# Graph attention and a mixture of experts: the router's logits out of the projections

## The chip, the cores and the metric

The kernel runs on one core of a Trainium2 chip. The metric is the device time of one execution in microseconds (us), taken as the median of several runs.

## The reference, cut to what matters

```python
edge_index = jnp.stack([src, dst])
x = x + gnn(layernorm(x), edge_index, W, att_src, att_dst, bias)
x = x + moe(layernorm(x), router_w, w1, b1, w2, b2)

def gnn(x, ...):                                   # H = 8 heads, C = 256
    h = (x @ W).reshape(N, H, C)
    a_src, a_dst = einsum('nhc,hc->nh', h, att_src), einsum('nhc,hc->nh', h, att_dst)
    e = leaky_relu(a_src[src] + a_dst[dst], 0.2)
    alpha = softmax of e over the edges of one dst
    return segment_sum(h[src] * alpha, dst).mean(axis=heads) + bias

def moe(tokens, ...):                              # 8 experts, the best 2 of each row
    logits = tokens @ router_w.T
    rw, re = top_k(softmax(logits), 2), normalised
    return sum over e of combine[:, e] * (gelu(tokens @ w1[e] + b1[e]) @ w2[e] + b2[e])
```

N = 3125 nodes of D = 256 floats, 50,000 edges sorted by dst, all in 32-bit floats. The second layernorm's mean and rstd are those of the row after the first part, x1 = x + bias + mean over heads of the projections.

## The kernel before, in words

Nodes stand in 25 tiles of 128 rows, edges in 392 blocks of 128. Blocks are sorted by dst, so the sums of a tile of nodes come from a stretch of blocks. The projection by W is put behind the sum over edges: for every node and head the kernel sums alpha times the normalised x (256 numbers), and multiplies by W once, at the end. The order of the work on each engine is written out by hand in five programs (PE, DVE, ACT, POOL, SP); semaphores tie them together. `link` chains DVE instructions that follow from one another.

**Start.** SP loads x in seven transfers (L534 to L537) and stores zeros to starts_table (L539). ACT's queue loads W and the attention vectors. DVE makes the sums of W times attention vector (sum_va, L1401), PE their mean over D (mean_va, L927), DVE subtracts it (center_va, L1411). PE turns x tile by tile (turn_x, L919), and multiplies it by va: first for src (score(0), L932), later for dst. DVE scales by the rows' rstd (scale_scores, L1416), SP stores rows and scores as node_table (L570, L573).

**Gathers and sums, 57.56 to 656.6 us.** POOL gathers the node rows of each block (L740, 392 times), and in between sends the dst scores (L793) and reads start rows (L796). DVE makes the softmax, PE adds blocks into nodes (L978), ACT takes the sums out of PSUM and stores them in agg_table. POOL's last gather ends at 608.6, the last sums at 656.6.

**Projection, 656.6 to 853.2 us.** For tile t: SP loads the raw sums (load_raw, L603, 1.6 MB into one of three buffers; it waits for over_part(t-2) and own_part(t-3), since the buffer must be free). DVE adds what neighbouring pieces share (over_part(t), L1799 and L1804), ACT copies the rest (own_part(t), L1284). PE multiplies by W: 16 products of 128x128 by 128x256 into one PSUM bank (project(t), L1103), written into a bank that add_node(t-4) has left. DVE adds the result to x (add_node, L1815) and takes statistics (L1818). After five tiles DVE normalises them (normalise, L1822 to L1836) into tn, rows that POOL later sends to the experts' lists.

PE turns the normalised rows (turn_tn, L1114), ACT copies them out of PSUM (copy_tT, L1290), and PE multiplies them by router_w (router, L1123). After five tiles DVE subtracts the row's maximum (shift_logits, L1849 and L1850), ACT takes exp (L1294), DVE picks two experts (L1857 to L1891), PE counts rows per expert (positions(q), L1131 to L1133), DVE makes places (places_in_lists, L1896 to L1907), and POOL sends the rows (L840). DVE's program in this stage, for each t, is: over_part(t+2), then picks, places, or after tile 16 the counting of the jobs, then add_node(t), then normalise if five are whole. Tiles are taken from the last to the first in x_all (rows_of(t)).

Turns and router products are spread over the projections by turned_after(t): two tiles of rows behind most projections, the rest behind the last of a five. The last five tiles' rows are turned between the first expert jobs.

**Experts, 853 to 1013 us.** 56 jobs of up to 128 rows: load rows, turn (L1150), two products (L1162, L1178), result (results(j), L2044), and POOL adds it to the output (L854). The first 11 jobs work on the rows of the first ten tiles, while the last rows are still on their way.

Of the kernel before, what the change touches and what calls it, by code (L numbers as in the profile page):

```python
# [13 lines left out]
P = 128  # L14
# [13 lines left out]
BLK = 128  # L28
# [36 lines left out]
def gat_moe_kernel(nc, x, src, dst, W, att_src, att_dst, gnn_bias, router_w, w1, b1, w2, b2, out):  # L65
# [68 lines left out]
    with ExitStack() as ctx:  # L134
# [7 lines left out]
        RING = ROOM * ROW  # L142
        ring = sb("ring", [P, RING])
        rows = ring[0:BLK, :].rearrange("p (s d) -> p s d", d=ROW)

        o = 0
        xn = ring[:, o:o + TILES * D].rearrange("p (t d) -> p t d", d=D)
        o += TILES * D
        W_in = ring[:, o:o + 2 * H * C].rearrange("p (k n) -> p k n", k=2)
        o += 2 * H * C  # L150
# [6 lines left out]
        xT = ring[:, o:o + TILES * D].rearrange("p (t d) -> p t d", d=D)  # L157
        o += TILES * D
        reach_junk, first_home_bc, last_home_bc = (ring[:, o + n * NB:o + (n + 1) * NB] for n in range(3))
        o += 3 * NB  # L160
        assert o <= RING
# [7 lines left out]
        at_raw0 = at_W + 2 * H * C  # L169
        at_x = (first_of[GROUPS - 2] + SLOT0) % ROOM * ROW  # L170
        at_agg0 = at_x + TILES * D
        assert at_w1 + 4 * D <= at_W and at_raw0 + 2 * RAW <= at_x and at_agg0 + AGG <= RING
        assert at_x <= (first_of[WHOLE - 1] + SLOT0) % ROOM * ROW + GB * ROW
        x_all = ring[:, at_x:at_x + TILES * D].rearrange("p (t d) -> p t d", d=D)
        W_sb = ring[:, at_W:at_W + 2 * H * C].rearrange("p (k n) -> p k n", k=2)
# [132 lines left out]
        va = sb("va", [P, 2, 2 * H])  # L308
# [15 lines left out]
        node_half = sb("node_half", [P, 2 * TILES])  # L324
        counted = sb("counted", [P, 2 * TILES])
        block_of = sb("block_of", [P, TILES])
        block_at = sb("block_at", [P, TILES])
# [24 lines left out]
        router_sb = sb("router_sb", [P, 2, NX])  # L352
# [48 lines left out]
        def alphas_in_bank(g):  # L401
# [19 lines left out]
        dst_ready, first_bc_done, last_row_done = sem("dst_ready"), sem("first_bc_done"), sem("last_row_done")  # L421
        xn_ready, xT_done, xT_ready, score_done, score_ready = (
# [27 lines left out]
        tr_done, tT_ready, logit_done, shift_ready, exp_ready = (  # L450
            sem("tr_done"), sem("tT_ready"), sem("logit_done"), sem("shift_ready"), sem("exp_ready"))
        in_b2, fills_ready, filled = sem("in_b2"), sem("fills_ready"), sem("filled")
        taken_ready, pos_done, slots_ready = sem("taken_ready"), sem("pos_done"), sem("slots_ready")
        logits_read = sem("logits_read")
# [19 lines left out]

        def turned_bank(t):

            return bank[4 + t % 2] if t < TILES - UNROLL else bank[(7, 5)[t % 2]]

        def turned_after(t):

            each = {t0: 2 for t0 in range(UNROLL, TILES - UNROLL)}
            done = 0
            for i in range(UNROLL, t + 1):
                whole = i // UNROLL * UNROLL
                n = min(whole - done, each.get(i, 3))
# [1655 lines left out]
```

## Time and profile before

| | |
|---|---|
| runs shown | 1019.93, 1159.93, 1015.24 us; median 1019.93 |
| span of the profiled execution | 1013.5 us |
| its mean granted TensorE clock | 0.812 |
| busy share | PE 66%, DVE 66%, POOL 65%, ACT 35% |
| first gather of node rows | 57.56 us |
| end of the gathers | 608.6 us |
| projection | 656.6 to 853.2 us |

The profiled execution is one execution of its own; its time is its span and a few microseconds around it, and the clean runs lie 1.7 and 6.4 us above that span. Times of rows are microseconds from the start of the span. PEld is the load of weights, which overlaps PE; SPq and DVEq are the sequencers of SP and DVE. A row's square bracket tells how long the engine was idle before it and what ended that.

### The profile page before, as it was taken

How to read it: one execution, taken by the hardware profiler on the slowest of the kernel's cores; microseconds unless marked ns; L12 is line 12 of the kernel's file. 1: busy time of each engine (PE TensorE's matmuls, PEld its weight loads, DVE VectorE, ACT ScalarE, POOL GpSimd, SP SyncE). 2: the span in 40 equal slices, each digit the busy share in tenths (PEclk: the TensorE clock that was granted, in tenths of full speed). 3: DMA queues.
4: the chain of work that ended last, by engine and by line, in shares of the span. 5: the costliest groups of instructions: out<-in, count | busy, mean ns of one | idle time of the engine just before them, and what ended most of it. 6: DMA issues, size and time to landing. Idle time of an engine off the chain costs nothing.

```text
span 1013.5 us, 15559 instructions
## 1 busy us (share of the span) xinstructions
PE 669.1 (66%) x3740; PEld 603.6 (60%) x3741; DVE 673.9 (66%) x1844; ACT 355.2 (35%) x831; POOL 657.5 (65%) x705
## 2 busy tenths in 40 slices
PE   3982012428546275472656678699999998678996
PEld 2981001327545275472656678688888886567995
DVE  6988318727657276573876778557768868765663
ACT  3730003347645364241332210123322232335674
POOL 5777777777777777777777770244063275557876
PEclk9555555579877797776977798799999999789998
DMA  9634153578867677565664555098985772366874
GB/s 348 212 94 95 24 119 105 165 228 266 264 201 238 214 247 225 164 194 160 186 190 136 165 174 228 29 389 311 340 334 192 289 245 71 86 130 106 133 129 58
DMA packets 96984, 189.61 MB, mean 187 GB/s; under 512 B 24743, under 2 KB 54802, under 8 KB 95804
## 3 DMA queue, kind: packets, MB, share of 16 engines
q0 software_dynamic: 31680, 70.52, 28.6%
q1 hardware_dynamic: 50256, 72.93, 21.3%
q10 hardware_dynamic: 14960, 45.16, 11.5%
q8 instruction: 34, 0.56, 0.2%
q14 instruction: 54, 0.44, 0.1%
HBM read 124.74 MB, written 64.74 MB: 187 GB/s over the span
## 4 chain that ended last, share of the span: by engine, by line
PE 29%; DVE 23%; POOL 21%; issue 12%; DMA 8%; ACT 3%; DVEq 1%; ACTq 1%; POOLq 1%; SPq 0%; PEld 0%; PEldq 0%
POOL ring L740 17%; PE banks L1103 10%; PE banks L978 8%; PE banks L1162 3%; PE banks L1178 3%; POOL starts_table L793 2%; DMA ring<-agg_table 2%; DMA ring<-node_table,idx 2%; DMA out<-ring 2%; PE banks L932 2%; DVE arena L1379 2%; DVE ring L1804 1%; DVE arena L1684 1%; ACTq L1250 1%; ACT arena L1264 1%
## 5 line engine op out<-in xcount | busy, mean ns | idle before, releaser
L740 POOL DMA_INDIRECT ring<-node_table,idx x392 | 396.6, 1012 | 121.4 <-issue 113.8
L978 PE MATMUL banks<-arena,ring 128*128 128x160 f32 x1568 | 258.2, 329 | 36.7 <-ACT banks L1270 19.1
L978 PEld LDWEIGHTS banks<-arena,ring 128*128 128x128 f32 x1568 | 246.8, 213 | 48.7 <-issue 48.5
L1264 ACT COPY arena<-banks 128x400 f32<-128x400 f32 x200 | 88.4, 493 | 312.6 <-PE banks L978 196.6
L1103 PE MATMUL banks<-ring 128*128 128x256 f32 x544 | 120.5, 381 | 0.0
L854 POOL DMA_INDIRECT out<-ring x56 | 89.8, 1603 | 33.2 <-DMA out<-ring 16.8
L1103 PEld LDWEIGHTS banks<-ring 128*128 128x128 f32 x544 | 102.5, 190 | 13.4
L1754 DVE TENSOR_TENSOR arena<-hot,banks 128x640 f32<-128x640 f32 x84 | 64.6, 814 | 37.4 <-PE banks L978 35.1
L985 PE MATMUL banks<-ident,edge_e 128*128 128x128 f32 x25 | 7.1, 415 | 111.2 <-DVEq L1655 111.2
L1162 PEld LDWEIGHTS banks<-ring 128*128 128x128 f32 x448 | 61.1, 201 | 19.0 <-DVE ring L2020 15.8
L1162 PE MATMUL banks<-ring 128*128 128x128 f32 x448 | 63.7, 288 | 12.7 <-DVE ring L2020 12.3
L985 PEld LDWEIGHTS banks<-ident,edge_e 128*128 128x128 f32 x25 | 3.9, 201 | 113.1 <-DVEq L1655 113.1
L840 POOL DMA_INDIRECT slot_table<-arena,slots x50 | 54.6, 1093 | 14.5 <-issue 13.7
L1178 PE MATMUL banks<-arena,ring 128*128 x224 | 61.7, 400 | 1.6 <-issue 1.6
L835 POOL COPY arena<-tags 128x3 f32<-128x3 f32 x25 | 3.6, 195 | 84.5 <-DVEq L1908 84.5
L1103 PE MATMUL banks<-ring,arena 128*128 128x256 f32 x256 | 57.0, 381 | 0.0
L1268 ACT COPY banks<-zeros 128x400 f32<-128x400 f32 x100 | 50.4, 504 | 11.5 <-ACT arena L1264 10.3
L1647 DVE TENSOR_TENSOR edge_z<-ring,arena 128x384 f32<-128x384 f32 (+2 forms) x9 | 4.3, 477 | 74.8 <-DMA ring<-node_table,idx 74.7
L1103 PEld LDWEIGHTS banks<-ring,arena 128*128 128x128 f32 x256 | 48.3, 190 | 6.4
L2044 DVE SCALAR_TENSOR_TENSOR ring<-banks,job_w,ring 128x256 f32<-128x256 f32 x56 | 27.1, 484 | 36.1 <-PE banks L1178 21.4
L1270 ACT COPY banks<-zeros 128x400 f32<-128x400 f32 x100 | 49.7, 497 | 0.0
L1178 PEld LDWEIGHTS banks<-arena,ring 128*128 128x128 f32 x224 | 40.2, 200 | 6.8 <-issue 2.9
(411 smaller groups left out, 1175.7 us busy)
## 6 DMA issues: line engine op xcount, KB each, us to landing
agg_table<-arena ACTq DMA_DIRECT2D x100, 400.0 KB
ring<-agg_table SPq DMA_DIRECT2D x25, 1600.0 KB, 8.5
ring<-slot_table SPq DMA_DIRECT2D x56, 130.0 KB, 2.6
ring<-node_table,idx POOLq DMA_INDIRECT x392, 3.0
ring<-in_x SPq DMA_DIRECT2D x8, 640.0 KB, 12.6
arena<-in_L_ffn_w SPq DMA_DIRECT2D x16, 256.0 KB, 8.6
node_table<-ring SPq DMA_DIRECT2D x5, 640.0 KB, 5.2
ring<-in_L_gnn_W ACTq DMA_DIRECT2D x1, 2048.0 KB, 9.1
```

Of the source, the lines that this page charges most:

```text
L740: pool.indirect_dma_start(rows[:, slot_of(b), :], None, node_table, bass.IndirectOffsetOnAxis(idx[:, b:b + 1], 0)).then_inc(got[got_of(g)] ...
L840: pool.indirect_dma_start(slot_table, bass.IndirectOffsetOnAxis(slots[:, k, t:t + 1], 0), tn[t % TN_RING], None).then_inc(sent[t % TN_RING ...
L854: pool.indirect_dma_start(out, bass.IndirectOffsetOnAxis(xs[j % XS_RING][:, D:D + 1].bitcast(I32), 0), ybuf[j % Y_RING], None, bounds_chec ...
L978: m = pe.matmul(columns[:, k, bass.ds(at * (UNIT * H), SPREAD * H)], lhs[:, k * P:(k + 1) * P], weights, start=False, stop=True, skip_grou ...
L1103: m = pe.matmul(bank[proj_bank(t)][:, 0:D], aggt[t % AGG_RING][:, k * H + h, :], W_sb[:, k, h * C:(h + 1) * C], start=(k == 0 and h == 0), ...
L1162: m = pe.matmul(h_bank[j % 2][:, f * P:(f + 1) * P], w1_now[j % 2][:, k, f * P:(f + 1) * P], xsT[j % 2][:, k, :], start=(k == 0), stop=(k ...
L1178: m = pe.matmul(y_bank[j % 2][:, 0:D], h_sb[j % 2][:, f, :], w2_sb[:, bass.ds(e, 1), f, :].rearrange("p e n -> p (e n)"), start=(f == 0), ...
L1264: act.copy(stage[j][:, k * SLOTS * H:(k + 1) * SLOTS * H], views[k]).then_inc(drained, 1)
L1268: act.copy(views[0], zeros[:, 0:1].to_broadcast([P, SLOTS * H]))
L1270: act.copy(views[1], zeros[:, 0:1].to_broadcast([P, SLOTS * H])).then_inc(acc_free, 1)
L1754: dve.tensor_tensor(spread[:, s:s + QUAD, :].rearrange("p s (d h) -> p s d h", h=H), hot[:, q * QUAD:(q + 1) * QUAD, :].unsqueeze(3).to_br ...
L2044: dve.scalar_tensor_tensor(ybuf[j % Y_RING], y_bank[j % 2][:, 0:D], job_w[j % 3][:, 1:2], b2_now[j % 3], ALU.mult, ALU.add).then_inc(y_rea ...
```

## The change

The router's logits of a normalised row are rstd * (x1 . r - mean * sum(r)), and x1 . r is x . r + bias . r + the mean over heads of (sums @ (W_h @ r)). The kernel after the change makes these three parts and no longer turns and multiplies the normalised rows:

- x . r: router_w is loaded as 8 rows (r_rows), PE turns it to rT beside va, and the score products have 16 columns in place of 8. DVE keeps the part in x_logits.
- W_h @ r: PE turns W in 32 pieces, ACT copies them, PE multiplies them by rT: 8 more columns per head, which DVE places in W_sb. Each projection then has 264 columns, and add_node adds the 8 new ones to x_logits.
- bias . r and sum(r) come from two more small products; shift_logits has three more instructions for mean and rstd.

turn_tn, router and copy_tT are gone, and with them their semaphores. router_sb is no longer loaded. W_sb is loaded in two transfers with rows of 1 KB, and load_raw(1) also waits for one more block, since its buffer lies elsewhere. Two modulo operations of PE's register work are masks now, and POOL's waits in the adding of results have one more mask. The last shift_logits stands ahead of results(0).

```diff
+            sp.dma_start(r_rows, router_w).then_inc(in_router, 16)
             sp.wait_ge(zero_ready, 1)
...
-            sp.dma_start(W_sb[:, :, :], W.rearrange("(k p) n -> p k n", p=P)).then_inc(in_proj_w, 16)
+            for k in range(2):
+                sp.dma_start(W_sb[:, k, :, 0:C], W[k * P:(k + 1) * P, :].rearrange("p (h n) -> p h n", h=H)).then_inc(in_proj_w, 16)
             load_raw(0)
+            sp.wait_ge(block_done, first_of[GROUPS - 2] + 2)
             load_raw(1)
...
+            pool.wait_ge(w_router_done, 1)
             pool.wait_ge(target_scores_stored, 16)
...
-                at_least = [pool.snap(new[j - i - 1] + (y_landed(i) - 16)) for i in ahead]
+                at_least = [pool.snap((new[j - i - 1] & 16) + (y_landed(i) - 16)) for i in ahead]
...
             def score(a, t):
+                n = (H + NX, H)[a]
                 for k in range(2):
-                    m = pe.matmul(bank[a][:, t * H:(t + 1) * H], xT[:, t, k * P:(k + 1) * P], va[:, k, a * H:(a + 1) * H],
-                                  start=(k == 0), stop=(k == 1))
+                    m = pe.matmul(bank[a][:, t * n:(t + 1) * n], xT[:, t, k * P:(k + 1) * P],
+                                  va[:, k, 0:H + NX] if a == 0 else va_of[1][:, k, :], start=(k == 0), stop=(k == 1))
...
+            pe.wait_ge(in_router, 16)
+            for k in range(2):
+                pe.transpose(bank[1][:, H + k * NX:H + (k + 1) * NX], r_rows[:, k * P:(k + 1) * P], ident[0:NX, 0:NX])
             mean_va(0)
...
+            pe.wait_ge(blocks_counted, 2 * TILES)
+            pe.wait_ge(x_logits_kept, 1)
+            W_PARTS = 2 * H * C // P
+            for i in range(W_PARTS // 4):
+                if i >= 2:
+                    pe.wait_ge(wT_ready, i - 1)
+                for n in range(4):
+                    k, c = divmod(4 * i + n, W_PARTS // 2)
+                    m = pe.transpose(bank[(0, 2)[i % 2]][:, n * P:(n + 1) * P], W_in[:, k, c * P:(c + 1) * P], ident[:, :])
+                m.then_inc(w_turned, 1)
+            for i in range(W_PARTS // 2):
+                pe.wait_ge(wT_ready, i // 2 + 1)
+                for f in range(2):
+                    pe.matmul(bank[7][:, i * NX:(i + 1) * NX], wT[:, 2 * i + f, :], rT[:, f, :], start=(f == 0), stop=(f == 1))
...
-                        mid = pe.snap((at_homes // 256) % 128 + 1)
+                        mid = pe.snap(((at_homes // 256) & 127) + 1)
...
-                        m = pe.matmul(bank[proj_bank(t)][:, 0:D], aggt[t % AGG_RING][:, k * H + h, :], W_sb[:, k, h * C:(h + 1) * C],
+                        m = pe.matmul(bank[proj_bank(t)][:, 0:CN], aggt[t % AGG_RING][:, k * H + h, :], W_sb[:, k, h, :],
...
                 project(t)
-                for i in turned_after(t):
-                    turn_and_route(i)
...
+                if a == 0:
+                    dve.tensor_copy(x_logits[:, :, :], got_scores[:, :, H:]).then_inc(x_logits_kept, 1)
...
+            dve.tensor_copy(W_sb[:, :, :, C:].rearrange("p k h e -> p (k h) e"), w_router.rearrange("p (i e) -> p i e", e=NX))\
+                .then_inc(w_router_placed, 1)
             over_part(0)
...
             results(0)
-            shift_logits(LAST_Q)
```

The order of work shows the change at three places. First PE at the end of a cycle of five, before: the last turns and router products behind one projection, then project, positions(2) and the next project (L1103 is project, L1114 the turns, L1123 the router, L1132 and L1133 positions).

```order
L1123 MATMUL banks<-router_sb,tT 128x8 [waits tT_ready]
L1123 MATMUL banks<-router_sb,tT 128x8
L1123 MATMUL banks<-router_sb,tT 128x8 [waits tT_ready]
L1123 MATMUL banks<-router_sb,tT 128x8
L1103 MATMUL banks<-ring 128x256 [waits y1_ready,agg_own,agg_over]
L1103 MATMUL banks<-ring 128x256 x15
L1103 MATMUL banks<-ring 128x256 [waits y1_ready,agg_own,agg_over]
L1103 MATMUL banks<-ring 128x256 x15
L1132 MATMUL banks<-pick_tmp,before_me 128x40 [waits taken_ready]
L1133 MATMUL banks<-taken,ones_sq 128x40
L1103 MATMUL banks<-ring,arena 128x256 [waits y1_ready,agg_own,agg_over]
```

And after the change, where L1126 is project and L1135 and L1136 are positions:

```order
L1126 MATMUL banks<-ring,arena 128x264 [waits y1_ready,agg_own,agg_over]
L1126 MATMUL banks<-ring,arena 128x264 x15
L1126 MATMUL banks<-ring 128x264 [waits y1_ready,agg_own,agg_over]
L1126 MATMUL banks<-ring 128x264 x15
L1126 MATMUL banks<-ring 128x264 [waits y1_ready,agg_own,agg_over]
L1126 MATMUL banks<-ring 128x264 x15
L1135 MATMUL banks<-pick_tmp,before_me 128x40 [waits taken_ready]
L1136 MATMUL banks<-taken,ones_sq 128x40
L1126 MATMUL banks<-ring,arena 128x264 [waits y1_ready,agg_own,agg_over]
```

Between two positions PE now has nothing but projections; its waits for tn and tT are gone, and positions still waits for taken_ready, which DVE's picks give.

Second, the start of PE's program, before: the last of the first turns of x, the mean of va, the next turns.

```order
L919 MATMUL banks<-ident,ring 128x128 [waits in_x1]
L919 MATMUL banks<-ident,ring 128x128
L927 MATMUL banks<-va,ones_sq 128x8 [waits va_summed,idx_ready,dst_ready]
L927 MATMUL banks<-va,ones_sq 128x8
L919 MATMUL banks<-ident,ring 128x128 [waits in_x1,xT_ready,va_ready]
L919 MATMUL banks<-ident,ring 128x128
```

After (L943 turns the router's rows):

```order
L917 MATMUL banks<-ident,ring 128x128 [waits in_x1]
L917 MATMUL banks<-ident,ring 128x128
L943 MATMUL banks<-ident,ring 128x8 [waits in_router,idx_ready,dst_ready]
L943 MATMUL banks<-ident,ring 128x8
L925 MATMUL banks<-va,ones_sq 128x8 [waits va_summed]
L925 MATMUL banks<-va,ones_sq 128x8
L917 MATMUL banks<-ident,ring 128x128 [waits in_x1,xT_ready,va_ready]
L917 MATMUL banks<-ident,ring 128x128
```

The two turns of router_w stand ahead of the mean, and the wait in_router with them; all that stands behind them on PE waits too.

Third, DVE in the projection stage, from an add_node (L1815, L1818) over an over_part (L1799, L1804) to the beginning of the picks (L1849), before:

```order
L1815 SCALAR_TENSOR_TENSOR ring<-banks,ring 128x256 [waits proj_done,bias_added]
L1818 BN_STATS stats<-ring 128x6 [waits y1_ready]
L1799 TENSOR_TENSOR ring<-ring 128x8x18 [waits proj_done,raw_in1,dve_chain]
L1804 TENSOR_TENSOR ring<-ring 128x8x3x18
L1799 TENSOR_TENSOR ring<-ring 128x8x18
L1804 TENSOR_TENSOR ring<-ring 128x8x3x18
L1849 TENSOR_REDUCE row<-banks 128x5 [waits logit_done]
L1850 TENSOR_TENSOR logits<-banks,row 128x40 [waits dve_chain]
```

And after, where add_node is L1812, L1814 and L1817, over_part L1796 and L1801, and shift_logits begins at L1846:

```order
L1812 SCALAR_TENSOR_TENSOR x_logits<-banks,x_logits 128x8 [waits proj_done,bias_added]
L1814 SCALAR_TENSOR_TENSOR ring<-banks,ring 128x256 [waits dve_chain]
L1817 BN_STATS stats<-ring 128x6 [waits y1_ready]
L1796 TENSOR_TENSOR ring<-ring 128x8x18 [waits proj_done,raw_in1,dve_chain]
L1801 TENSOR_TENSOR ring<-ring 128x8x3x18
L1796 TENSOR_TENSOR ring<-ring 128x8x18
L1801 TENSOR_TENSOR ring<-ring 128x8x3x18
L1846 TENSOR_TENSOR probs<-mean,rT_sum 128x40
L1847 TENSOR_TENSOR probs<-x_logits,probs 128x40 [waits dve_chain]
L1848 TENSOR_TENSOR probs<-probs,rstd 128x40 [waits dve_chain]
L1849 TENSOR_REDUCE row<-probs 128x5 [waits dve_chain]
L1850 TENSOR_TENSOR logits<-probs,row 128x40 [waits dve_chain]
```

L1812 and L1846 to L1848 are new; before, L1849 waited for logit_done of PE.

## Rows read from the trace of the kernel before

**Rows 1.** Spans and mean granted clock of the core.
```profile
core 0: 1013.5 us, clock 0.812
```

**Rows 2.** Timelines of four engines, start (start us, us, what, [idle before]).
```profile
23.02 0.58 PE L927 MATMUL banks<-va,ones_sq 128*128 128x8 f32 x4 [1.83 <-DVEq L1406]
...
18.61 0.33 SPq L539 DMA_DIRECT2D starts_table<-arena  x1
...
52.13 0.36 DVE L1416 TENSOR_TENSOR score_all<-banks,rstd 128x200 f32<-128x200 f32 x1 [2.41 <-PE banks L932]
...
57.56 1.00 POOL L740 DMA_INDIRECT ring<-node_table,idx  x1 [0.30 <-issue]
```

**Rows 3.** Windows, start (length; busy PE, PEld, DVE, ACT, POOL; clock, DMA share, GB/s).
```profile
28.00:30.00 2.00, 2.00 (x11) 2.00 (x11) 2.00 (x8) 2.00 (x8) 1.55 (x5) 0.50 0.85 277
30.00:32.00 2.00, 2.00 (x12) 2.00 (x11) 2.00 (x8) 2.00 (x9) 1.70 (x2) 0.50 0.17 55
```

**Rows 4.** Page, costliest groups, POOL's gathers.
```profile
L740 POOL DMA_INDIRECT ring<-node_table,idx x392 | 396.6, 1012 | 121.4 <-issue 113.8
```

**Rows 5.** Windows in the projection stage and behind it.
```profile
725.00:750.00 25.00, 23.90 (x121) 20.59 (x120) 19.36 (x63) 5.72 (x10) 14.63 (x23) 1.00 0.74 268
750.00:775.00 25.00, 24.89 (x124) 22.00 (x123) 18.44 (x58) 7.86 (x10) 4.32 (x11) 1.00 0.73 272
...
862.00:866.00 4.00, 3.99 (x26) 3.82 (x25) 2.61 (x13) 2.27 (x4) 3.31 (x5) 0.72 0.31 104
...
866.00:876.00 10.00, 5.32 (x24) 4.53 (x23) 7.99 (x41) 2.97 (x6) 3.04 (x8) 0.67 0.29 65
```

**Rows 6.** Timeline of PE, projection stage and its end.
```profile
722.93 7.07 PE L1103 MATMUL banks<-ring 128*128 128x256 f32 x32
...
729.84 0.31 PE L1132 MATMUL banks<-pick_tmp,before_me 128*128 128x40 f32 x2
...
738.31 0.75 PE L1114 MATMUL banks<-ident,arena 128*128 128x128 f32 x4 [0.96 <-DVE arena L1836]
...
739.68 7.15 PE L1103 MATMUL banks<-ring,arena 128*128 128x256 f32 x32
...
746.67 0.38 PE L1114 MATMUL banks<-ident,arena 128*128 128x128 f32 x2
...
747.98 7.15 PE L1103 MATMUL banks<-ring 128*128 128x256 f32 x32
...
754.97 0.38 PE L1114 MATMUL banks<-ident,arena 128*128 128x128 f32 x2
...
756.28 7.15 PE L1103 MATMUL banks<-ring 128*128 128x256 f32 x32
...
838.38 0.42 PE L1132 MATMUL banks<-pick_tmp,before_me 128*128 128x40 f32 x2 [1.39 <-DVEq L1882]
...
861.77 0.44 PE L1114 MATMUL banks<-ident,arena 128*128 128x128 f32 x2 [2.40 <-DVE arena L1836]
```

**Rows 7.** Timeline of DVE, the same stage.
```profile
746.94 0.42 DVE L1815 SCALAR_TENSOR_TENSOR ring<-banks,ring 128x256 f32<-128x256 f32 x1 [1.65 <-PE banks L1103]
...
749.61 0.74 DVE L1799 TENSOR_TENSOR arena<-ring 128x144 f32<-128x144 f32 x1 [1.78 <-DMA ring<-agg_table]
...
755.24 0.42 DVE L1815 SCALAR_TENSOR_TENSOR ring<-banks,ring 128x256 f32<-128x256 f32 x1 [1.51 <-PE banks L1103]
...
759.12 0.43 DVE L1799 TENSOR_TENSOR ring<-ring 128x144 f32<-128x144 f32 x1 [2.99 <-DMA ring<-agg_table]
...
763.19 0.20 DVE L1861 TENSOR_TENSOR pick_tmp<-probs,row 128x40 f32<-128x40 f32 x1
```

**Rows 8.** Chain of waits, end of the projection stage.
```profile
822.72 8.98 DMA ring<-agg_table
```

**Rows 9.** Timeline of PE and DVE, ahead of the reads.
```profile
109.23 0.58 PE L963 MATMUL banks<-ident,step_cols 128*1 128x128 f32 x2 [25.99 <-DVEq L1584]
...
147.32 0.17 DVE L1605 COPY arena<-start_rows 98x8 f32<-98x8 f32 x1 [34.93 <-DMA arena<-starts_table]
```

More of the change, by code:

```diff
@@ L160, in gat_moe_kernel @@
         o += 3 * NB
-        assert o <= RING
+        r_rows = ring[0:NX, o:o + D]
+        o += D
+        assert o <= RING and 2 * H * C <= SLOT0 * ROW
         AGG = 2 * H * P
@@ L473, in y_landed @@
             return 16 * (j // Y_RING + 2)
[L475 to L485, printed above, removed]
-                if i == t:
-                    return range(done, done + n)
-                done += n
-            return range(0)
         POSITIONS_AFTER = {2 * UNROLL - 1: 0, 3 * UNROLL - 1: 1, 4 * UNROLL - 1: 2, 5 * UNROLL - 3: 3}
@@ L960, in _ @@
             m.then_inc(home_bc_done, 1)
+            pe.wait_ge(blocks_counted, 2 * TILES)
[12 more added lines that the diff above has]
+                    pe.matmul(bank[7][:, i * NX:(i + 1) * NX], wT[:, 2 * i + f, :], rT[:, f, :], start=(f == 0), stop=(f == 1))
+            pe.wait_ge(bias_rows_ready, 1)
+            for k in range(2):
+                m = pe.matmul(bank[7][:, 2 * H * NX:2 * H * NX + H + NX], ones_sq[:, :], va[:, k, 0:H + NX], start=(k == 0), stop=(k == 1))
+            m.then_inc(w_router_done, 1)
             pe.wait_ge(step_cols_ready, 1)
@@ L1236, in _ @@
                 count_blocks(n)
+            for i in range(2 * H * C // (4 * P)):
+                act.wait_ge(w_turned, i + 1)
+                act.copy(wT[:, 4 * i:4 * i + 4, :].rearrange("p i n -> p (i n)"), bank[(0, 2)[i % 2]]).then_inc(wT_ready, 1)
             for h in range(H):
@@ L1514, in _ @@
             scale_scores(1)
+            dve.wait_ge(in_router, 16 * 2)
+            for k in range(2):
+                link(dve.tensor_scalar(va[:, k, 0:H], rT[:, k, :], bias_cols[:, k:k + 1], None, ALU.mult))
+            dve.sem_inc(bias_rows_ready, 1)
             link(dve.tensor_copy(extras[:, :], extra_f[:, :]))
@@ L1846, in shift_logits @@
                 tiles, r, rev = parts(q)
-                dve.wait_ge(logit_done, tiles.stop)
-                scores = bank[6][:, 0:UNROLL * NX].rearrange("p (s e) -> p s e", e=NX)
+                scores = probs[:, :, :]
+                link(dve.tensor_tensor(scores, bc(mean[:, tiles], UNROLL), rT_sum[:, :].unsqueeze(1).to_broadcast([P, UNROLL, NX]), ALU.mult))
+                link(dve.tensor_tensor(scores, x_logits[:, TILES - tiles.stop:TILES - tiles.start, :][:, ::-1, :], scores, ALU.subtract))
+                link(dve.tensor_tensor(scores, scores, bc(rstd[:, tiles], UNROLL), ALU.mult))
                 link(dve.tensor_reduce(r[0], scores, AX_X, ALU.max))
@@ L2090, in _ @@
             normalise(TILES - 2, 2)
+            shift_logits(LAST_Q)
             results(0)
-            shift_logits(LAST_Q)
             first_pick(LAST_Q)
```

122 lines of the change are left out of this document (51 added, 71 removed).

## The prediction

> **What bounds the kernel now.** I read the spans first, then the page's groups, the windows of 25 us, the timelines of PE and DVE, and last the chain of waits. The profiled execution spans 1013.5 us at a mean granted clock of 0.812 [rows 1]. There are three long stages with different limits, and the reader should see a different engine lead in each.
>
> The start, until the first gather of node rows at 57.56, is a chain: PE takes the mean of W·att at 23.02, turns x and makes the scores, which DVE scales at 52.13; they go to the node table, and POOL gathers from it [rows 2]. From there to 608.6 POOL sets the pace: 392 gathers of 1.012 us, and 113.8 of its 121.4 us of waiting are plain issue time [rows 4]. Whatever moves the start moves this whole stage.
>
> The stage from 656.6 to 853.2 projects 25 tiles (196.6 us). By busy time PE leads: 24.89 of 25 us in one window, against DVE's 18.44 [rows 5]. By waits it is less clear. In the cycle of five tiles that ends near 780 PE waits for DVE's normalised rows once, 0.96 us [rows 6]; DVE waits for PE twice (1.65 and 1.51), and right behind each it waits again, 1.78 and 2.99, for the raw sums that SP loads from agg_table [rows 7]. The chain of waits goes through such a load, 8.98 us at 822.72, then through ACT's own_part [rows 8]. SP issues raw(t) when DVE has finished over_part(t-2), and over_part(t) waits for it: a loop of DVE and DMA with no matmul in it, except through buffers that come free.
>
> **The change, part by part.**
>
> *Projection, PE.* A tile is 16 products of 256 columns: from 722.93 to 729.84, 6.91 us [rows 6]. At 264 columns it is 6.91 x 264/256 = 7.13: +0.216, over 25 tiles +5.4. What goes are turns and router products: 738.31 to 739.68, 746.67 to 747.98, 754.97 to 756.28, which is 1.37 + 1.31 + 1.31 = 4.0 per five tiles of rows, and the wait of up to 0.96 [rows 6]. Over the four cycles that is 16 of work and about 3 of waits. Were PE the bound all along, the stage would take -19 + 5.4 = -14. That is rival A.
>
> *Projection, DVE.* Each add_node gets one more instruction, 128x8 out of PSUM; each pick of five tiles gets three more of 128x40. A 128x40 takes 0.20 [rows 7]; with the gap to the next I take 0.235 for it and 0.21 for the 128x8. 5 x 0.21 + 3 x 0.235 = 1.75 per five tiles, 8.8 over the stage.
>
> *Which of them decides.* PE, lighter by 4.0 - 1.1 per cycle, runs ahead. DVE's two waits for PE shrink, but the wait for raw sums behind each grows by as much, since that load was issued behind an over_part that stands ahead of both. Once PE's lead is used up by this, DVE's work alone sets the cycle, and that grows by 1.75, of which the raw waits swallow what lies between an over_part and the next load. Walking through the cycles with these durations I get normalise(4) later by 0.8, (9) by 1.7, (14) by 3.0, (19) by 3.5; these four are estimates, and in the cycle with the job counting (after tile 16) DVE hardly waits, so nothing is swallowed. From over_part(22) on the chain is the load, own_part, exps, picks, positions(3), project(23) and (24) [rows 8]: +0.7 for the new instructions of the picks and +0.43 for two wider tiles, less some 1.1 of router work that stood between. I take +3.5; the same walk with quicker loads gives +1, with slower ones +4.5, and -14 is the lower end.
>
> *PE's new waits.* PE will stand still where it used to turn rows: some 5 us before positions(1), 3 before positions(2), 8 before positions(3), where it waited 1.39 [rows 6]. The granted clock, 1.00 in the windows of this stage, fell to 0.72 and 0.67 in 862 to 876, after PE had waited 2.40 at 861.77 [rows 5, 6]. A tile at the lower level, 1.2 GHz, takes 6.9 us longer; a stall may be followed by part of one. Behind positions(1) and (2) PE's lead hides most of it. I take +1, bounds 0 and +21.
> The Trainium skill, "TensorE: Matmul & The Clock Gate", section on HAM oscillation, says that waits between bursts of products throttle the array again, so that each next burst starts cold. The trace agrees at 862 to 876; by that rule each of the three stalls is followed by a slow stretch, which is rival C.
>
> *The start.* router_w's load goes on SP's queue where the store of starts_table stands at 18.61, ahead of that store and behind the loads of x, and PE waits for it before the mean at 23.02 [rows 2]. The DMA engines are at 0.85 at 28 to 30 and at 0.17 after it [rows 3]. The store behind it is 1.57 MB, some 5 us at 277 GB/s, so the loads of x end near 25, and these 8 KB with them: 25.5 (bounds: 21.2, which costs nothing, and 30, which costs 7). Then two turns and the copy of rT, 0.6 together: the mean's product starts near 26.1 and the scores 3.2 later. DVE copies x_logits, 128x200, 0.36 as L1416 itself takes [rows 2], ahead of the sums that POOL's gather waits for. Of the 3.5 about 1.0 may be slack between the stored scores and POOL's look-ups, and some of the turning of x can fill the wait: I take +2.2 at the first gather, and as POOL seldom waits for others until 608.6 [rows 4], +2.2 behind that stage.
>
> *Turning W.* 32 turns and 34 small products on PE, 8 copies on ACT. Two turns took 0.58 at 109.23, two small products 0.58 at 23.02: 66 x 0.29 = 19 us [rows 2, 9]. They lie in PE's idle 25.99 us before 109.23 and the stretch behind it, DVE's five small instructions in its 34.93 before 147.32 [rows 9]. POOL's new wait, ahead of the read of the start rows, comes some 30 us behind that work, with nothing on POOL delayed. Cost 0; without cover it would be 19. The copy of the router columns into W stands ahead of over_part(0), where DVE waits for PE's last blocks; W itself comes in rows of 1 KB, 50 us before its use: 0.
>
> *Register work and the end.* PE's modulo per four blocks becomes a mask, more instructions of shorter length: 0, bound 1. POOL's adding of expert outputs gets a mask per awaited job beside waits for landed data: +0.3, bounds 0 and 2. At the tail, PE's turns that waited until 861.77 are gone [rows 6], and the maximum of the logits follows the last normalise, but results(0) stands ahead of the first pick: -0.3, bounds -1.3 and 0.
>
> **Sum.** +2.2 (start) +3.5 (projection) +1 (clock) +0.3 (POOL) -0.3 (tail) = +6.7: a span of about 1020. The clean runs shown are 1015.24 and 1019.93, which is 1.7 and 6.4 above the profiled span; with 4 to 5 around it the time is 1025. Against the median shown, 1019.93, that is half a per cent more, and a measurement of this kernel tells about 2%, 20 us.
>
> **The rivals.**
> A, PE is the bound. For it: the busy shares [rows 5]. Against it: the waits for raw sums directly behind DVE's waits for PE [rows 7]. It gives -14 in the stage, +2.2 at the start and -0.3 at the tail: 1013.5 - 12 and 4.5 around it, about 1006.
> The Trainium skill, "Perfetto Trace Analysis", section Identifying the Most-Contended Engine, says to relieve first the engine of the highest occupancy, TensorE judged by its weight loads (here 22.00 of 25 us, DVE 18.44). By that page A is the likeliest case; the order of the waits makes me put it second.
> B, little moves. The router row lands early, loads are quick, the clock stays, part of PE's lead does reach DVE: 0 at the start and -4 to +1 behind it, 1014 to 1020.
> C, slower: the clock. If each of the three stalls is followed by one slow tile, +6.9 each, and PE's lead doesn't hide them, +21, with the other terms +5.7: about 1045. It decides from the point where a slow stretch outlasts the lead of 5 to 8 us. For it: the fall at 862 [rows 5]. Against it: the window of 725 to 750 kept 1.00 through the wait of 0.96 [rows 5, 6].
>
> **How the numbers follow.** Forecast (+2 to +14; 1020 to 1033) 0.56, A (1001 to 1010) 0.20, B 0.14, C 0.07, something else, such as a longer start, 0.03. The forecast stands at 1025; the range that leaves out two in ten is 1004 to 1037. Faster by over 2% (below 999.5) 0.04, slower by over 2% (above 1040.3) 0.07, within 2% 0.89.
>
> **What would show it.** Start: the first gather near 59.8. PE: a wait of several us before positions(1) and positions(3) where now there are 0 and 1.39, tiles of 7.1 us. DVE: waits for raw sums longer, waits for PE near 0. It would be wrong if the stage takes under 190 us (then A), if the first gather is at 57.6, or if the windows of the stage show a clock under 0.95 (then C).

## The result and the profile after

The kernel after takes 1022.45 us (median of 11 runs), the kernel before 1018.46 in the same series: a ratio of 1.0038, 95% interval 1.0021 to 1.0055, so some 4 us slower. One of the 11 runs of the kernel before took 1159.93 us, in a slow state; it is in the median and not in the ratio. The forecast was 1025, +6.7 over the profiled span. The profiled execution spans 1016.9 us, 3.4 more than [rows 1]. Both profiled executions are among the quickest of their kernels (by its span about 1015.2 us where the median is 1018.46, and 1018.63 where it is 1022.45), so a difference of 1 or 2 us between two profiles can be one execution's own.

The start, in the timelines of PE and POOL after the change (start us, us, what, idle before):

```profile
24.88 0.35 PE L943 MATMUL banks<-ident,ring 8*128 8x8 f32 x2 [4.23 <-DMA ring<-in_L_ffn_router_w]
25.16 1.02 PE L925 MATMUL banks<-va,ones_sq 128*128 128x8 f32 x4
...
59.75 0.94 POOL L737 DMA_INDIRECT ring<-node_table,idx  x1 [2.84 <-DVEq L1386]
```

PE waits 4.23 us for router_w, and the mean's product stands at 25.16 in place of 23.02. The first gather is at 59.75 in place of 57.56 [rows 2], +2.19. On the way there DVE scales the scores at 54.65 in place of 52.13, +2.52.

The projection stage as one window, from the first product of project to the start of the last, in the kernel before and then in the kernel after (length; busy PE, PEld, DVE, ACT, POOL; clock, DMA share, GB/s):

```profile
656.60:853.00 196.40, 191.39 (x944) 166.94 (x943) 144.74 (x442) 54.34 (x76) 82.14 (x121) 1.00 0.75 277
```

```profile
655.90:855.30 199.40, 186.92 (x824) 157.58 (x822) 153.64 (x482) 47.58 (x56) 86.25 (x123) 0.97 0.75 274
```

The reader sees three things. The stage is 3.0 us longer, though PE has 4.5 us less to do. DVE has 8.9 us more. And the stage begins at 655.9, where it began at 656.6: of the 2.2 us lost at the start nothing is left in this pair of profiles. Behind the stage 161.6 us are left, before 160.5: +1.1. So -0.7 + 3.0 + 1.1 = 3.4.

PE's waits in the stage, in its timeline after the change; they answer to the waits of 0.96 and 1.39 in [rows 6]:

```profile
766.60 0.39 PE L1134 MATMUL banks<-taken,ones_sq 128*128 128x8 f32 x2 [1.94 <-DVEq L1881]
767.29 16.17 PE L1126 MATMUL banks<-ring 128*128 128x264 f32 x64
...
807.01 0.41 PE L1135 MATMUL banks<-pick_tmp,before_me 128*128 128x40 f32 x2 [2.04 <-DVEq L1881]
807.48 9.06 PE L1126 MATMUL banks<-ring,arena 128*128 128x264 f32 x32
...
838.27 0.65 PE L1135 MATMUL banks<-pick_tmp,before_me 128*128 128x40 f32 x2 [7.43 <-DVEq L1881]
839.14 8.98 PE L1126 MATMUL banks<-ring,arena 128*128 128x264 f32 x32
```

PE stands still ahead of positions(1), (2) and (3), and the row behind each wait is 1.6 to 1.8 us longer than rows of the same length elsewhere in the stage (7.28 for one tile, 14.55 for two; 16.17 is two tiles). The granted clock behind the waits shows it, here in the 3 us behind the longest; behind the other two it is 0.56 (767 to 770) and 0.55 (808 to 811), where it was 1.00 before PE stood still:

```profile
838.00:841.00 3.00, 2.73 (x8) 2.36 (x9) 2.64 (x10) 0.00 (x0) 0.00 (x0) 0.50 0.30 80
```

At 838.27 the cause of the wait can be followed back on ACT and DVE:

```profile
831.15 1.90 ACT L1275 COPY ring<-ring 128x448 f32<-128x448 f32 x2 [10.61 <-DMA ring<-agg_table]
832.95 0.24 ACT L1281 ACTIVATE logits<-logits 128x40 f32<-128x40 f32 x1
```

```profile
828.90 0.41 DVE L1850 TENSOR_TENSOR logits<-probs,row 128x40 f32<-128x40 f32 x1
833.28 0.20 DVE L1856 TENSOR_REDUCE row<-logits 128x5 f32<-128x40 f32 x1 [3.96 <-ACT logits L1281]
```

DVE has the logits of the fourth five ready at 829.3. ACT could take their exp at once, but its program has own_part(24) first, which waits for the raw sums until 831.15. Before the change this order held DVE up almost as long:

```profile
833.83 0.20 DVE L1857 TENSOR_REDUCE row<-logits 128x5 f32<-128x40 f32 x1 [3.30 <-ACT logits L1294]
```

But PE then had turns and router products to do and waited only 1.39 us for the picks [rows 6]. positions(3) itself stands at 838.27 after the change and at 838.38 before it: PE's 7.43 us are its lead, which ends in this wait.

### The profile page after: what moved, and what is told of

Same layout as the page of the kernel before. It is cut to its first block, busy times and chain, and to the rows that moved or that the text cites. A ratio compares the mean times of both kernels' runs of the same rounds, so it can differ in the third digit from the quotient of the medians.

```text
span 1016.9 us, 16065 instructions
## 1 busy us (share of the span) xinstructions
PE 684.6 (67%) x3692; PEld 614.7 (60%) x3693; DVE 687.7 (68%) x1892; ACT 351.3 (35%) x814; POOL 654.6 (64%) x705
## 4 chain that ended last, share of the span: by engine, by line
DVE 25%; PE 24%; POOL 23%; issue 12%; DMA 9%; SPq 2%; ACT 1%; POOLq 1%; DVEq 1%; ACTq 0%; PEld 0%; PEldq 0%
POOL ring L737 20%; PE banks L1000 8%; PE banks L1126 5%; PE banks L1171 3%; PE banks L1158 3%; DMA ring<-agg_table 3%; DMA out<-ring 3%; POOL starts_table L790 2%; PE banks L931 2%; DVE ring L1801 2%; DMA ring<-node_table,idx 2%; DVE arena L1359 2%; SPq L528 1%; PE banks L1146 1%; PE banks L917 1%
## 5 line engine op out<-in xcount | busy, mean ns | idle before, releaser
L737 POOL DMA_INDIRECT ring<-node_table,idx x392 | 393.4, 1003 | 124.1 <-issue 114.5
L1000 PE MATMUL banks<-arena,ring 128*128 128x160 f32 x1568 | 261.4, 332 | 38.2 <-ACT banks L1261 18.8
L1000 PEld LDWEIGHTS banks<-arena,ring 128*128 128x128 f32 x1568 | 251.0, 216 | 49.2 <-issue 48.6
L1126 PE MATMUL banks<-ring 128*128 128x264 f32 x544 | 124.8, 390 | 1.1 <-DVE ring L1801 1.1
L1126 PEld LDWEIGHTS banks<-ring 128*128 128x128 f32 x544 | 104.0, 192 | 19.7 <-DVE ring L1801 2.0
L1158 PEld LDWEIGHTS banks<-ring 128*128 128x128 f32 x448 | 61.8, 204 | 26.2 <-DVE ring L2021 23.3
L1126 PE MATMUL banks<-ring,arena 128*128 128x264 f32 x256 | 61.7, 402 | 0.0
L1275 ACT COPY ring<-ring 128x448 f32<-128x448 f32 x30 | 28.9, 1012 | 82.8 <-DMA ring<-agg_table 82.8
L1126 PEld LDWEIGHTS banks<-ring,arena 128*128 128x128 f32 x256 | 50.8, 199 | 9.2
```

The costliest lines, as they stand in the source:

```text
L737: pool.indirect_dma_start(rows[:, slot_of(b), :], None, node_table, bass.IndirectOffsetOnAxis(idx[:, b:b + 1], 0)).then_inc(got[got_of(g)] ...
L1000: m = pe.matmul(columns[:, k, bass.ds(at * (UNIT * H), SPREAD * H)], lhs[:, k * P:(k + 1) * P], weights, start=False, stop=True, skip_grou ...
L1126: m = pe.matmul(bank[proj_bank(t)][:, 0:CN], aggt[t % AGG_RING][:, k * H + h, :], W_sb[:, k, h, :], start=(k == 0 and h == 0), stop=(k == ...
L1158: m = pe.matmul(h_bank[j % 2][:, f * P:(f + 1) * P], w1_now[j % 2][:, k, f * P:(f + 1) * P], xsT[j % 2][:, k, :], start=(k == 0), stop=(k ...
L1275: a = act.copy(to[:, k, :, :, OVER:HOME], raw[t % RAW_RING][:, :, k, OVER:HOME, :].rearrange("p v n h -> p h v n"))
```

## The experiments

They ran in four series, each on one chip with the kernel before beside it: e1, e4, e5 and e6 on one, e2, e3, e8 and e10 on another, e11 to e13 on a third, e14 on a fourth. The chips differ: beside the result and beside e11 to e13 the kernel before takes 1018 us, beside the first eight runs 1145, beside e14 1155. So I read two things of each run: the ratio to the kernel before of the same chip, and the length of the projection stage in its profile.

Each length comes from one profile. For the kernels like before it hardly depends on the chip (196.4, e5 195.3, e13 195.3). For those like after, which do the same work in this stage, it spreads more: 199.4, e1 201.5, e8 201.8, e12 202.2. Cutting the stage at the start of positions(3) shows where each run gains or loses (us):

| run | start of the stage to positions(3) | from there to the end | stage |
|---|---|---|---|
| before | 181.8 | 14.6 | 196.4 |
| e5, before with the masks | 180.7 | 14.6 | 195.3 |
| e4, e5 without the turns | 178.7 | 16.7 | 195.4 |
| e6, e5 with DVE's additions | 183.6 | 14.6 | 198.2 |
| after | 182.4 | 17.0 | 199.4 |
| e1 | 183.4 | 18.1 | 201.5 |
| e8, after again | 183.8 | 18.0 | 201.8 |
| e12 | 184.5 | 17.7 | 202.2 |
| e11, after with PE kept at work | 182.5 | 15.0 | 197.5 |

**e4 and e5: PE's relief by itself.** e5 is the kernel before with the register masks; e4 is e5 without the turns, ACT's copies and the router.

```diff
-                for i in turned_after(t):
-                    turn_and_route(i)
...
-                scores = bank[6][:, 0:UNROLL * NX].rearrange("p (s e) -> p s e", e=NX)
+                scores = tn_all[:, at:at + UNROLL, 0:NX]
```

> The kernel before with the change's register masks alone (the two modulo operations of PE per four blocks, one more mask per awaited job on POOL); nothing else differs. My theory, that the change's cost lies in the projection stage and the start: time as before, within 1.5 us, the gathers end at the same time as before (608.6 us). Rival, that the masks gave back what the start lost in the gather stage: the sums end 2 to 3 us earlier than 656.6.

> As e5, and the turns of the normalised rows, their copies on ACT and the router products are left out; DVE takes the first eight columns of the normalised rows as logits, so the routing is another one. This relieves PE exactly as the change does, without the wider products and without anything on DVE. Theory, DVE and the loads of raw sums bound the stage: 0 to -3 us, and DVE's waits for raw sums grow while its waits for PE go. Rival, PE is the bound: -14 us or more.

Measured: e5 1144.96 us, ratio 1.0014 (0.9984 to 1.0044); e4 1142.25 us, ratio 0.999 (0.9956 to 1.0024). The stage is 195.3 us in e5 and 195.4 in e4. Here are the waits of the stage (us in total, times, longest), first e5, then e4:

```profile
DVE ring L1799 <- DMA ring<-agg_table: 14.6, 6, 3.6
...
DVE ring L1815 <- PE banks L1103: 8.4, 5, 2.5
DVE arena L1799 <- DMA ring<-agg_table: 8.4, 3, 4.1
...
DVE row L1857 <- ACT logits L1294: 2.7, 4, 1.8
```

```profile
DVE ring L1784 <- DMA ring<-agg_table: 18.4, 6, 4.2
...
DVE arena L1784 <- DMA ring<-agg_table: 10.6, 3, 4.6
...
PE banks L1133 <- DVEq L1865: 8.3, 2, 8.1
...
DVE row L1840 <- ACT logits L1286: 6.3, 4, 5.2
```

DVE's wait for PE, 8.4 us, is gone. Its waits for raw sums go from 23.0 to 29.0, and that for the exp from 2.7 to 6.3: together 9.6 more. PE, with some 10 us less to do, waits for DVE instead. Rival A, -14, falls.

The unchanged length hides two things, though: e4 is 2.0 us quicker up to positions(3) and 2.1 slower behind it. There PE has waited 8.07 us, where it waited 0.26 in e5, and the next tile takes 8.89 us in place of 7.15:

```profile
963.21 0.65 PE L1133 MATMUL banks<-pick_tmp,before_me 128*128 128x40 f32 x2 [8.07 <-DVEq L1865]
963.66 0.63 PE L1134 MATMUL banks<-taken,ones_sq 128*128 128x40 f32 x2
964.09 8.89 PE L1104 MATMUL banks<-ring,arena 128*128 128x256 f32 x32
```

The granted clock of the stage is 0.96 in e4. So, by one profile against one, PE's relief is worth 2 us, and the clock takes them back. The masks by themselves cost nothing that can be measured.

**e6: DVE's additional instructions by themselves**, on e5.

```diff
                 dve.wait_ge(proj_done, t + 1)
+                link(dve.scalar_tensor_tensor(spare_logits[:, rows_of(t), :], bank[proj_bank(t)][:, 0:NX], 1.0 / H, spare_logits[:, rows_of(t), :],
+                                              ALU.mult, ALU.add))
...
+                link(dve.tensor_tensor(spares, spares, bc(mean[:, tiles], UNROLL), ALU.mult))
+                link(dve.tensor_tensor(spares, spares, bc(mean[:, tiles], UNROLL), ALU.subtract))
+                link(dve.tensor_tensor(spares, spares, bc(rstd[:, tiles], UNROLL), ALU.mult))
```

> As e5, with the change's additional DVE instructions of the projection stage alone: one 128x8 out of PSUM per add_node (25) and three of 128x40 per pick of five tiles, on a scratch of their own, results unused. Theory, DVE is in the path: +2 to +5 us. Rival, PE is the bound and DVE has room: within 1 us of e5.

Measured: ratio 1.0058 (1.0025 to 1.0092), 4.8 us above e5 by the medians; the stage 198.2, +2.9, all of it ahead of positions(3). DVE is busy 6.3 us more there (150.9 against 144.6), and the rest goes into its idle time. DVE is in the path.

**e8: the kernel after again, and e2: without the 25 additions to the logits.**

> The kernel after, unchanged, as the measure for the runs beside it, since another chip than the first one ran the last four (before: 1145.5 us). If the chip is again one on which the stage of gathers is long: theory, the projection stage is 3 to 3.5 us longer than in the kernel before (199.4 against 196.4 in the first pair), whatever the chip; what the start and the gathers do is open, and could be of either sign there.

```diff
-                link(dve.scalar_tensor_tensor(x_logits[:, rows_of(t), :], bank[proj_bank(t)][:, D:CN], 1.0 / H, x_logits[:, rows_of(t), :],
-                                              ALU.mult, ALU.add))
```

> The kernel after without the 25 additions of the projections' eight columns to x_logits (L1812): the logits lack the part of the graph attention, so the routing is another one. Theory, DVE is in the path: the stage is 1 to 3 us shorter than the kernel after's. Rival, these small instructions are hidden by the waits for raw sums: under 0.5 us.

Measured: e8 1134.87 us, and here the ratio is 0.9896 (0.987 to 0.9921): on this chip the change makes the kernel 1.0% faster. Its stage is 201.8 us, so what is gained lies ahead of it (last section). Part of what sets it apart from the first profile of the same kernel is one load of raw sums: ahead of the picks of the second five DVE waits for it 3.65 us at 874.05 in e8 and 4.13 at 762.43 in e12, where it was 2.22 at 758.14, and PE's wait for positions(1) goes from 1.94 to 3.40 and 3.88.

e2: ratio 0.9897, the stage 198.2, 3.6 shorter than e8's, where 1 to 3 were expected. With the spread between profiles of the kernel after, this supports that these additions are in the path, but does not give their price to 1 us. Its total is no lower than e8's: the last part, with another routing, takes 166.3 us against 161.6.

**e3: the exp ahead of own_part(24).**

```diff
             for t in range(TILES):
+                if t == TILES - 3:
+                    exps(TILES // UNROLL - 2)
                 if t + 2 < TILES:
                     own_part(t + 2)
```

> The kernel after with ACT's exp of the fourth five (exps(3)) ahead of own_part(24) in place of behind it; before the change this order would have gained little, since the router's products came only just before. DVE waited 3.96 us for it at 833.28. Theory: DVE's wait at the last picks of the stage falls to under 0.5, PE's wait ahead of positions(3) from 7.43 to about 3.5, and the stage and the time are 3 to 4 us less than the kernel after. Rival, own_part(24) is then late for project(24), or the wait only moves to bring_w1 and the job rows: under 1 us less.

Measured: the stage 199.3 us, 2.5 less than e8's; DVE's longest wait for the exp falls from 3.9 to 0.4, PE's longest wait from 7.4 to 5.6. Ratio 0.9877 (0.9855 to 0.99), not told from e8's. DVE's wait fell as expected, PE's by 1.8 us where 4 were expected; the stage gained 2.5 us where 3 to 4 were expected, in one profile against one.

**e11: PE kept at work in its waits.**

```diff
+                if q < 4:
+                    for _ in range((0, 4, 4, 15)[q]):
+                        pe.matmul(bank[6][:, 0:D], ones_sq[:, :], W_sb[:, 0, 0, 0:D], start=True, stop=True)
                 pe.wait_ge(taken_ready, q + 1)
```

> The kernel after with 4, 4 and 15 products of 128x256 into a PSUM bank that nobody reads, ahead of the waits of positions(1), (2) and (3), so that PE does not stand still there (1.7, 1.7 and 6.5 us of work in waits of 1.9, 2.0 and 7.4). In the kernel after the tiles behind these waits took 8.98 and 9.06 us and 16.17 for two, where 7.12 each is the rule: 1.9 us each. Theory, this is the fallen clock and it lies in the path: the granted clock of the stage goes from 0.97 to 1.00 and the stage is 2 to 4 us shorter (199.4 and 201.8 in the two profiles of the kernel after). Rival, only the one behind positions(3) counts: 1.9 us. Rival, none: the same time.

Measured: 1020.38 us, ratio 1.003 (1.0014 to 1.0046), which is not told from 1.0038. The stage of this run as one window, and PE at positions(3), where L1133 are the added products:

```profile
655.90:853.40 197.50, 192.07 (x869) 162.42 (x868) 151.37 (x478) 47.62 (x56) 81.41 (x121) 1.00 0.75 276
```

```profile
830.84 6.64 PE L1133 MATMUL banks<-ring,ones_sq 128*128 128x256 f32 x30
838.40 0.41 PE L1138 MATMUL banks<-pick_tmp,before_me 128*128 128x40 f32 x2 [0.92 <-DVEq L1884]
...
838.86 7.37 PE L1126 MATMUL banks<-ring,arena 128*128 128x264 f32 x32
```

The granted clock goes from 0.97 to 1.00 and the tile behind positions(3) from 8.98 to 7.37 us; the small products of positions(3) ahead of it take 0.46 in place of 0.87. The stage is 1.9 shorter, all of it behind positions(3) (15.0 against 17.0). That is the price of one slow stretch, not of three: after positions(1) and (2) PE's time comes back as new waits ahead of the next projections (1.05, 0.43 and 1.46). The second outcome named holds.

**e1: router_w loaded first of all.**

```diff
         def _(sp):
+            sp.dma_start(r_rows, router_w).then_inc(in_router, 16)
             for a, ends_of in ((1, dst), (0, src)):
```

> The kernel after with the load of router_w issued first on SP's queue, ahead of the edges and of x, so that the wait ahead of the mean of va is gone. Theory: the first gather starts near 57.9 in place of 59.75 and the time is 1.5 to 2.2 us less than the kernel after. Rival, the gather stage gives the start's delay back anyway (in the profile of the kernel after its sums ended 0.7 us earlier than before, despite the start): the first gather is early but the time is that of the kernel after, within 0.5 us.

Measured: 1136.19 us, ratio 0.9932 (0.9904 to 0.9961), on the chip of e4 to e6. It doesn't answer the question, since the move costs at least what it saves. The first row of PE's timeline, in e8 and then in e1, shows it:

```profile
12.33 1.54 PE L901 MATMUL banks<-ident,arena 98*128 98x98 f32 x8 [12.33 <-DVE arena L1369]
```

```profile
14.69 1.54 PE L901 MATMUL banks<-ident,arena 98*128 98x98 f32 x8 [14.69 <-DVE arena L1369]
```

The edges come 2.4 us later behind the new load (12.18 in e5, on the chip of e1), and the mean stands at 25.19, where e8 has 25.25. The first gather, expected near 57.9, is at 66.12, later than e8's 63.85. In e10 and e14, which carry the same move, it is at 66.4 and 66.7. A place behind the edges and ahead of x wasn't tried.

**e12: no turning of W.** The turns, products and copies of W go, and the columns are zero:

```diff
-                    m = pe.transpose(bank[(0, 2)[i % 2]][:, n * P:(n + 1) * P], W_in[:, k, c * P:(c + 1) * P], ident[:, :])
...
-            link(dve.tensor_copy(w_router, bank[7][:, 0:2 * H * NX]))
+            link(dve.memset(w_router, 0.0))
```

> The kernel after without the turning of W and the products with the router's rows (64 instructions of PE, 8 copies of ACT); the eight columns are zero, so the logits lack the part of the graph attention. On the first chip I expect no difference in the start or the gathers, within 1 us. On chips where the kernel before takes 1145 us and the first sums start at 257 us against 217 in the kernel after: theory, it is this additional work between 90 and 110 us that changes which waits of ACT and DVE fall into the slow grid there, and then the first sums start late again, near 257; rival, it is the missing load of router_sb: then they stay near 217.

Measured: 1027.52 us, ratio 1.0093 (1.0078 to 1.0107), slower than the kernel after. The gathers' stage ends 2.7 us later (658.6 against 655.9, from the same first gather), the projection takes 202.2 against 199.4 and the rest 164.8 against 161.6. The last may be due to the other routing, as in e2. The stage is as long as e1's and e8's, so it needs no cause in this edit. My "within 1 us" was wrong for the gathers. All five runs lie between 1027.2 and 1029.1, above every run of the kernel after, though the kernel has less to do: I have no mechanism for it. It ran on a chip where before takes 1018, so its question about the others stays open.

**e13: router_sb loaded late**, on e5.

> The kernel before with the change's register masks and with the two loads of router_sb (2048 elements of 4 bytes) issued late, ahead of the load of W for the projections, in place of 145 us. Nothing else differs. On the first chip: as before, within 1 us. On chips where the kernel before takes 1145 us: theory, the small loads are not the cause and the time stays at 1145, first sums at 257; rival, they are: then ACT's eight copies, 11.2 us apart there, come at once, and it gains 20 us or more up to the first sums.

Measured: 1017.41 us, ratio 0.9988 (0.9976 to 1.0). On this chip as expected, and it shows the small loads to cost the kernel before at most 2.4 us (the lower end of the interval); its question about the other chips stays open too.

**e10 and e14: the parts together.** e10 has x_all in rows of 264, e3 and e1; e14 has e11's products on top (4, 4 and 11). The move of e1 is in both, though e1 had not shown it to help.

```diff
-                link(dve.scalar_tensor_tensor(x_logits[:, rows_of(t), :], bank[proj_bank(t)][:, D:CN], 1.0 / H, x_logits[:, rows_of(t), :],
-                                              ALU.mult, ALU.add))
-                dve.scalar_tensor_tensor(x_all[:, rows_of(t), :], bank[proj_bank(t)][:, 0:D], 1.0 / H, x_all[:, rows_of(t), :], ALU.mult, ALU.add)\
+                dve.scalar_tensor_tensor(x_wide[:, rows_of(t), :], bank[proj_bank(t)][:, 0:CN], 1.0 / H, x_wide[:, rows_of(t), :], ALU.mult, ALU.add)\
```

> The kernel after with three things: rows of x_all are 264 wide and hold the logits in their last eight columns, so that one DVE instruction of 128x264 adds both (25 fewer); exps(3) stands ahead of own_part(24); router_w is loaded first of all. Theory: -1.5 to -3, -3 to -4 and -2 us, together 6 to 9 us less than the kernel after, so 2 to 5 us less than before where the first chip is concerned. Rival: the parts are not additive, since each frees DVE only for the wait for raw sums behind it; then 3 to 5 us less than after, about the time of before.

> The kernel after with everything that a run before has shown to help: one DVE instruction of 128x264 for the rows and the logits, exps(3) ahead of own_part(24), router_w loaded first of all, and 4, 4 and 11 products that nobody reads ahead of PE's waits at positions(1), (2) and (3). Theory, the terms add up: the projection stage, 199.4 us in the kernel after and 196.4 before, is 192 to 194, the first gather is at 57.6 to 58, and the time is 6 to 9 us less than the kernel after, so a ratio to before of 0.995 to 0.998. Rival, they don't, because each gives DVE only a longer wait for raw sums: the stage is 195 to 196 and the ratio 0.999 to 1.001. On a chip where the kernel before takes 1145 us the ratio is near 0.988 in either case, as those of the kernel after and its variants were there.

Measured: e10 1131.2 us, ratio 0.9888 (0.9865 to 0.9912), the stage 195.9, 5.9 less than e8's. The 6 to 9 us expected of the whole did not come: the ratio is not told from e8's. e14 1137.67 us where before takes 1155.29, ratio 0.9847 (0.9811 to 0.9884), the stage 193.1:

```profile
782.50:975.60 193.10, 190.15 (x860) 160.83 (x860) 149.69 (x456) 47.78 (x56) 82.73 (x121) 1.00 0.77 282
```

In the stage the terms about add up: 2.5 (e3), 3.6 (e2) and 1.9 (e11) are 8.0, and it is 8.7 us less than e8's, 3.3 less than the kernel before's 196.4. e14 beats the kernel before on such a chip, by 1.5%. Against the kernel after (0.9896, on another chip of that kind) the intervals overlap, and on the chip of the result it did not run. There it would be about at before's time or a little under it, with 3.3 us less in the stage, 1.1 more behind it, and if nothing of the start's delay is left behind the gathers; that is an estimate.

## Why the prediction was right

- **The start.** "I take +2.2 at the first gather": it was +2.19. The number is closer than the way to it. The mean's product came at 25.16, where 26.1 was forecast, and of the 3.5 us of delay some 1.3 were to be lost in slack; measured were 2.52 at the scaling of the scores, of which 0.3 was lost. Two errors of about 1 us cancel, which is luck. And "+2.2 behind that stage" was wrong: the stage of gathers ended at 655.9 in place of 656.6. In e11 it did so too (655.9), in e12 it ended at 658.6, in e13, with no delay at its start, at 657.3. The mean of one gather is 1003 ns after and 1012 before, and POOL's sum of them, 393.4 us in place of 396.6, holds what came back. Such differences need no change at the start: in e5 and e6, with the same start as before, the sums are 396.7 and 393.9. Why they were shorter here is not shown. This is the term that failed: +2.2 predicted, -0.7 measured.
- **The projection.** +3.5 for DVE and +1 for the clock, together +4.5; the pair of profiles has +3.0, those of e1, e8 and e12 have +6.2 to +6.9 over the 195.3 of e5 and e13. DVE's additional work was right (8.8 forecast, 8.9 measured). So was the mechanism that its wait for PE turns into one for raw sums, but not that it does so in full: 2.0 us of PE's relief reached the stage in e4, whose tiles are not wider. Up to positions(3) the parts are -2.0 for that relief and +2.9 for DVE's instructions (e6), together +0.9; the pair has +0.6. Behind positions(3) they are 2.0 for the slow stretch (e11; 2.1 in e4) and 0.43 for two wider tiles by the forecast's own estimate, together 2.4; the pair has +2.4. So in this pair the clock cost twice what was forecast and the rest 1.0 in place of 3.5: that the sum came out near is in part luck. Of e1, e8 and e12 these parts leave 3 to 4 us unexplained; one longer load of raw sums is part of it. The Trainium skill, "Perfetto Trace Analysis", section Identifying the Most-Contended Engine, would have chosen A, for which -14 was worked out; by e4 the order of the waits decides.
- **PE's waits.** 5, 3 and 8 us were expected, 1.94, 2.04 and 7.43 came. The fall of the clock is there: 0.97 over the stage, 0.50 to 0.56 in the 3 us behind each wait, which is the lower level, 1.2 GHz, for most of them, and tiles of 9.0 us. The Trainium skill, "TensorE: Matmul & The Clock Gate", section on HAM oscillation, says that waits between bursts of products make the next burst start slow. The trace agrees: waits of 1.94 and 2.04 us were each followed by 1.6 to 1.8 us of loss. Rival C's price of 6.9 us per stall was too high, since only part of a tile ran at the lower level, and two of the three were covered by PE's lead (e11).
- **Turning W**, at cost 0: it took PE from 85.94 to 105.14, 19.2 us where 19 was forecast, in PE's idle time. e12, without it, was slower, not faster.
- **The tail.** -0.3 and +0.3 for POOL's masks predicted, together 0; +1.1 measured for all that lies behind the last projection. Neither was tested alone; part of it is that the last picks wait for results(0), at 867.68 where they stood at 864.81, 2.9 later, with 2.3 of that from the stage's end.

The sum was +6.7 and +3.4 came in the profile, since the stage began 2.9 earlier than forecast and had 1.5 less, against 1.1 more behind it. The 4 to 5 us that the forecast put around the span are not one thing: each run lies 1.7 us above its own span, and the rest is what the profiled execution was quicker than the median. The measured 4 us lie inside the forecast's own range of +2 to +14. That holds for a chip like this one; on that of e8 the same change gave -1.0%, outside the range, for a reason that no rival names (last section).

## What to carry to other kernels

Before relieving an engine that is busy for 97% of a stage, look at what the engines that wait for it wait for next: if a transfer stands right behind, the relief mostly lengthens that wait (here 10 us of relief gave 2). Instructions added to an engine inside such a loop cost a part of their length (2.9 of 6.3 us). An engine that is relieved and then stands still may come back at a lower clock, and that took the 2 us away again. And when a change takes work away, look again at the order of the queues behind it: own_part(24) ahead of exps(3) held DVE up before and after the change, but only after it did PE have nothing else to do; putting exps(3) first gave 2.5 us there. On the kernel before it wasn't tried.

## What the runs showed of the hardware

Where the kernel before takes 1145 us, engines were seen to resume late from waits whose inputs were ready. ACT's copies of the scores (L1240), with all their inputs made by PE before 164, in e5, and the same copies in the kernel before on the chip of 1018 us:

```profile
186.80 0.81 ACT L1240 COPY arena<-banks 128x392 f32<-128x392 f32 x1 [10.38 <-issue]
198.00 0.81 ACT L1240 COPY arena<-banks 128x392 f32<-128x392 f32 x1 [10.38 <-remote]
209.20 0.81 ACT L1240 COPY arena<-banks 128x392 f32<-128x392 f32 x1 [10.38 <-remote]
```

```profile
152.02 0.84 ACT L1240 COPY arena<-banks 128x392 f32<-128x392 f32 x1 [0.21 <-PE banks L969]
153.13 0.84 ACT L1240 COPY arena<-banks 128x392 f32<-128x392 f32 x1 [0.27 <-PE banks L969]
```

They are 11.20 us apart, where 1.1 is usual. In e8 these copies came at 1.1 us again, but the first at 163.39 in place of 152.37 in the first profile of the same kernel. There chained instructions of DVE stood mostly 1.40 apart between 107 and 149, which used up 27.88 us that DVE otherwise waits for the start rows. 11.20 is 8 times 1.40. The first sums start at 257 us in e5 and at 217 in e8 (193 and 196 in the first pair of profiles), and that is where the kernel after gains on such chips; 21 of these 40 us are left when the projection begins (791.9 and 770.6). Whether this belongs to the chip or to something else that differed between the series is not shown. Which part of the change decides where these late resumptions fall is not shown: e12 and e13 were meant to tell, and ran on the other chip.
